# A recommendation tower in fp32: products of a batch in one run, dense inputs in unused places of the pairs, a small first load, most of the last batch's layer 1 ahead of its last products

## The chip, the cores and the metric

One Trainium2 chip, one of its cores. The metric is the device time of one execution in microseconds (us). "Before" ran three times: 175.21 us median, 174.92 to 176.21.

## What is computed

For each of 512 samples, 32 embedding rows of 256 numbers are looked up, all 496 dot products between them are taken, 16 dense inputs are appended, and three layers follow.

```python
e = jnp.stack([tbl_0[ids[:, 0]], ..., tbl_31[ids[:, 31]]], axis=1)   # 512 x 32 x 256
z = einsum('bnd,bmd->bnm', e, e)[:, iu, ju]                          # the pairs i < j, 496
h = jnp.concatenate([z, dense_ctx], axis=1)                          # 512 x 512
h = jnp.maximum(h @ W_top1 + b_top1, 0.0)                            # 512
h = jnp.maximum(h @ W_top2 + b_top2, 0.0)                            # 256
y = h @ W_top3                                                       # 1
```

## The kernel before

The samples are cut in 16 groups of 32 (n = 0 to 15); four groups are one batch b of 128 samples, for which the layers run.

**Look-ups.** The four smallest tables are looked up on PE: one-hot matmuls (`look_up`, L386) of the table's high and low parts; ACT keeps the result (`kept`). The other 28 tables are gathered by POOL: per group 7 indirect DMAs (L211) of 128 rows each, 112 in all, into a ring of 4 groups. The row numbers are `row_ids`, the sum (DVE, L219) of two arrays that one DMA loads at the start (`ids_sb`, L175, 112 KB).

**Fills.** `fill(n, u)` (L406), u = 0 to 3, transposes the rows of two gathers (one for u = 3) into one of three PSUM banks `xt_ps`; DVE (odd u) or ACT (even u) copies the bank to `xt`. PE waits for each gather by itself.

**Products.** `dots` (L429) multiplies the 32 x 32 products of the samples, eight bundles of four samples per group, each bundle four matmuls with 64 weight columns, alternately on the two halves of the array's columns. They go to `dots_ps`, two banks of two groups each ("a unit", v = n // 2). In the loop a group's products are spread: two bundles behind each of the next group's four fills (L502). Then `move` (DVE L246, 12 copies; ACT L311, 4) spreads a unit over `pairs`, which has the products as 8 columns j of 128 partitions x 128 samples.

**Layers.** For a batch, layer 1 is 4 chunks n of 128 outputs; each sums 8 matmuls over j (`pairs_part`, L440; weights 128 x 128, 128 sample columns) and one for the 16 dense inputs (`dense_part`, L435). Each fp32 matmul of the program stands as two records in the trace (the transposes as one). Layer 2 is 8 matmuls (L460), layer 3 is 2 (L468). The table `ROUND` says behind which fill of the 16 following ones each half chunk of layer 1 and the rest stand; `slots` turns group and fill into that number. All of it shares the bank `mlp_ps`.

**The end.** Behind the last fill stand half of layer 2 of batch 2, the products of group 15 in one run, the rest of layer 2 and layer 3; then the last batch: dense parts, then for k = 0 to 3 a chunk of layer 1 (16 records) followed by layer 2 of the chunk before it, each with a bank of its own; relu on ACT, the last relu on DVE (L272), layer 3, a copy (L326) and the store (L195). The moves of the last unit are made in two halves, one per group.

Each engine runs its own list in order; SP issues the loads, the weights into places of `small_sb` that the look-ups have left.

Of the kernel before, what the change touches and what calls it, by code (L numbers as in the profile page):

```python
# [32 lines left out]
DVE_QUADS = 3  # L33
FIRST = 4
# [6 lines left out]
def build_tower(nc, table, ids, small_tables, small_ids, chunk_rows, dense, w1, w1d, b1, w2, b2, w3, out):  # L41
# [7 lines left out]
    KR, CHUNKS = chunk_rows.shape  # L49
# [4 lines left out]
    with ExitStack() as ctx:  # L54
# [9 lines left out]
        ids_sb = sb("ids_sb", [P, 2, NM * GATHERS], I32)  # L64
# [3 lines left out]
        chunk_rows_sb = sb("chunk_rows_sb", [KR, CHUNKS])  # L68
# [14 lines left out]
        dense_sb = sb("dense_sb", [dense.shape[0], B])  # L83
        w1d_sb = sb("w1d_sb", [dense.shape[0], H1])
# [18 lines left out]
        last_l1_ps = [bank[:, 0:BLOCK] for bank in (*xt_ps, mlp_ps)]  # L103
        last_l2_ps = [bank[:, 0:BLOCK] for bank in found_ps[0]]
        last_l3_ps = found_ps[1][0][0:1, 0:BLOCK]
# [4 lines left out]
        chunk_rows_in = sem("chunk_rows_in")  # L110
# [43 lines left out]
        def moves(v, s, groups=(0, UNIT * GROUPS)):  # L154

            low_g, high_g = groups
            b, at = v // UNIT, s * Q + v % UNIT * UNIT * GROUPS
            for q in range(QUADS):
                col = s % 2 * N_FIELDS + q * JJ
                to = pairs[Q * q:Q * (q + 1), b % 2, :, at + low_g:at + high_g]  # L160
                source = dots_ps[v % 2][Q * s:Q * (s + 1), low_g:high_g, col:col + JJ]
# [11 lines left out]
        @block.sync  # L173
        def _(sp):
            sp.dma_start(ids_sb[:], ids).then_inc(ids_in, 16)  # L175
            for k in range(LOOKED_UP):
                if k:
                    sp.dma_start(small_ids_sb[:, k, :],
                                 small_ids[:, k, :].to_broadcast([KR, B])).then_inc(small_ids_in[k], 16)
                for c in range(0, CHUNKS, 2):  # L180
                    sp.dma_start(small_sb[:, k, c:c + 2, :],
                                 small_tables[k][:, c:c + 2, :]).then_inc(small_in[k][c // 2], 16)
            for to, source in ((b1_sb, b1), (b2_sb, b2), (w3_sb, w3)):
                sp.dma_start(to[:], source).then_inc(biases_in, 16)
            sp.dma_start(w1d_sb[:], w1d).then_inc(weights_in, 16)
            sp.dma_start(dense_sb[:], dense).then_inc(weights_in, 16)
# [6 lines left out]
            sp.dma_start(w2_sb[:], w2).then_inc(weights_in, 16)  # L193
            sp.wait_ge(y_ready, NB)
# [22 lines left out]
        def _(dve):  # L217
            dve.wait_ge(ids_in, 16)
            nc.vector.tensor_tensor(row_ids[:], ids_sb[:, 0, :], ids_sb[:, 1, :], ALU.add).then_inc(ids_ready, 1)  # L219
# [30 lines left out]
            dve.wait_ge(chunk_rows_in, 16)  # L250
            for two in range(TWOS):
                prepare(two)
            for f in range(len(FILL_BEHIND), FIRST * FILLS):
                take_xt(*divmod(f, FILLS))
# [21 lines left out]
        def _(act):  # L276
            act.dma_start(small_ids_sb[:, 0, :], small_ids[:, 0, :].to_broadcast([KR, B])).then_inc(small_ids_in[0], 16)
            act.dma_start(chunk_rows_sb[:], chunk_rows).then_inc(chunk_rows_in, 16)
# [70 lines left out]
            for n in range(FIRST + 1, NM):  # L349
                for u in range(FILLS):  # L350
                    take_xt(n, u)
                    if u == 1:
                        take_kept(n)
                        if n % 2 and n > FIRST + 1:
                            move((n - 3) // UNIT, range(DVE_QUADS, QUADS))
# [7 lines left out]
            v, b = NM // UNIT - 1, NB - 1  # L363
            move(v, range(DVE_QUADS, QUADS), (0, GROUPS))
            move(v, range(DVE_QUADS, QUADS), (GROUPS, UNIT * GROUPS))
            relu2(b - 1, loop_ps, range(N2))
# [7 lines left out]
        def _(pe):  # L374
# [35 lines left out]
            def dots(first, last):  # L410

                for n, g in (divmod(i, GROUPS) for i in range(first, last)):
                    v = n // UNIT
                    if g == 0:
                        on_act, on_dve = moved_fills(n, FILLS - 1)
                        pe.wait_ge(xt_act, on_act)
                        if on_dve:
                            pe.wait_ge(xt_dve, on_dve)
                        pe.wait_ge(kept_in_xt, n + 1)
                        if n % UNIT == 0 and v >= 2:  # L420

                            pe.wait_ge(moved_act, v - 1)
                            pe.wait_ge(moved_dve, v - 1)
# [7 lines left out]
                    if g == GROUPS - 1:  # L431
                        done.then_inc(dots_done, 1)

            def dense_part(b, n, banks, start=False):
                return nc.tensor.matmul(banks[n], w1d_sb[:, n * P:(n + 1) * P],  # L435
                                        dense_sb[:, b * BLOCK:(b + 1) * BLOCK], start=start, stop=not start)

            def pairs_part(b, n, columns, banks, start=True, stop=False):
                for j in columns:
                    done = nc.tensor.matmul(banks[n], w1_sb[:, j, n * P:(n + 1) * P], pairs[:, b % 2, j, :],  # L440
                                            start=(start and j == 0), stop=(stop and j == JJ - 1))
                return done

            def pairs_complete(b):
                more = b == NB - 1
                pe.wait_ge(moved_dve, 2 * (b + 1) + more)
                pe.wait_ge(moved_act, 2 * (b + 1) + more)

            def layer1_half(b, i):
                if i == 0:  # L450
                    pairs_complete(b)
# [3 lines left out]
                pairs_part(b, i // 2, range(i % 2 * JJ // 2, (i % 2 + 1) * JJ // 2), loop_ps)  # L455
                if i % 2:
                    dense_part(b, i // 2, loop_ps).then_inc(l1_done, 1)
# [33 lines left out]
            between = FIRST * FILLS - len(FILL_BEHIND)  # L491
            for i in range(between):
                fill(*divmod(len(FILL_BEHIND) + i, FILLS))
                dots(2 * GROUPS * i // between, 2 * GROUPS * (i + 1) // between)
            for u in range(FILLS):
                fill(FIRST, u)
                dots(2 * GROUPS + 4 * u, 2 * GROUPS + 4 * (u + 1))
            pe.wait_ge(weights_in, 16 * (JJ + 3))
# [5 lines left out]
            m, last = NB - 2, NB - 1  # L504
            dots((NM - 1) * GROUPS, NM * GROUPS)
            for u in range(FILLS):
                mlp(NM, u)
            for k in range(N1 - 1):
                dense_part(last, k, last_l1_ps, start=True)
            pairs_complete(last)  # L510
            pe.wait_ge(y_ready, last)
            dense_part(last, N1 - 1, last_l1_ps, start=True)
            for k in range(N1 + 1):
                if k < N1:
                    pairs_part(last, k, range(JJ), last_l1_ps, start=False, stop=True).then_inc(l1_done, 1)
                if k:
                    pe.wait_ge(h1_ready, last * N1 + k)
                    for n in range(N2):
                        layer2(n, k - 1, last_l2_ps)
            layer3(last, last_l3_ps)  # L520
# [62 lines left out]
```

## Time and profile before

| | us |
|---|---|
| median of three runs | 175.21 (174.92 to 176.21) |
| the profiled execution, its own time | 174.41 |
| its span, first to last instruction | 172.6 |
| PE busy | 153.7 (89%) |
| POOL busy | 110.5 (64%) |
| DVE, ACT busy | 68.6, 60.1 |

PE is TensorE's matmuls, PEld its weight loads, DVE VectorE, ACT ScalarE, POOL GpSimd, SP SyncE. Rows of a timeline are start us, duration us, engine, line, operation, output<-input, shapes, count, and in brackets the idle time before it and what ended it. Ends of matmuls are modelled: the records of a run overlap, so a run's pace is read from starts or from the chain of waits. The granted clock is TensorE's, as a share of 2.4 GHz.

### The profile page before, as it was taken

Reading aid. Unit: us, or ns where it says so; the run is one execution under the profiler, and the core shown is the slowest. Engines: PE = TensorE matmul, PEld = TensorE weight load, DVE = VectorE, ACT = ScalarE, POOL = GpSimd, SP = SyncE. Lnnn points to the kernel's source line nnn. Section 1 sums busy time; section 2 is a strip of 40 time slices with the busy share of each in tenths; the row PEclk is TensorE's granted clock in tenths of the full one; section 3 lists DMA queues with packets and bytes.
Section 4 is the critical chain, followed back from the end, with each engine's and each line's share of the span. In section 5 each row is a group of like instructions: output and inputs, shape, how many; then the busy total and the mean of one; then the engine's idle time right before and its main releaser. Section 6 shows DMA issues by size and latency. Waiting matters only on the chain.

```text
span 172.6 us, 4109 instructions
## 1 busy us (share of the span) xinstructions
PE 153.7 (89%) x1744; PEld 126.7 (73%) x1744; DVE 68.6 (40%) x186; ACT 60.1 (35%) x140; POOL 110.5 (64%) x118
## 2 busy tenths in 40 slices
PE   0199999998799999999998799999777999998993
PEld 0178888885588878888785587888545888887991
DVE  0699794600111892135216401640164015457000
ACT  2542848353623350114344121035251200453111
POOL 1677887777777777777777777777777777400000
PEclk9999999999789999999999999999999999999999
DMA  4999999643333334343433333333433333300000
GB/s 128 325 390 376 327 348 338 216 116 99 113 105 106 112 102 115 95 119 97 112 105 104 109 104 112 98 118 92 121 96 110 106 102 115 91 4 0 4 0 2
DMA packets 10356, 23.01 MB, mean 133 GB/s; under 512 B 2881, under 2 KB 3009, under 8 KB 10338
## 3 DMA queue, kind: packets, MB, share of 16 engines
q0 software_dynamic: 5376, 14.69, 29.0%
q1 hardware_dynamic: 4674, 7.79, 13.3%
q10 hardware_dynamic: 288, 0.27, 0.6%
q8 instruction: 14, 0.23, 0.5%
q14 instruction: 4, 0.03, 0.1%
HBM read 22.73 MB, written 0.00 MB: 132 GB/s over the span
## 4 chain that ended last, share of the span: by engine, by line
PE 67%; POOL 12%; DMA 6%; DVE 6%; issue 5%; ACT 4%; ACTq 0%; DVEq 0%
PE dots_ps L386 18%; PE mlp_ps L440 14%; PE dots_ps L429 12%; PE xt_ps L406 12%; POOL rows L211 12%; DVE pairs L246 4%; DMA rows<-table,row_ids 4%; PE xt_ps L440 3%; DMA chunk_rows_sb<-chunk_rows 3%; PE mlp_ps L435 3%; PE mlp_ps L460 2%; ACT h L317 1%; PE dots_ps L460 1%; ACT kept L289 1%; ACT xt L295 1%
## 5 line engine op out<-in xcount | busy, mean ns | idle before, releaser
L211 POOL DMA_INDIRECT rows<-table,row_ids x112 | 109.8, 980 | 37.7 <-issue 31.4
L295 ACT COPY xt<-xt_ps 128x512 f32<-128x512 f32 (+1 forms) x36 | 20.8, 577 | 81.4 <-PE xt_ps L406 81.4
L236 DVE COPY xt<-xt_ps 128x512 f32<-128x512 f32 (+1 forms) x28 | 15.6, 558 | 77.5 <-PE xt_ps L406 77.4
L406 PE MATMUL xt_ps<-ident,rows 128*128 128x128 f32 x224 | 39.4, 287 | 6.9 <-DMA rows<-table,row_ids 4.8
L429 PE MATMUL dots_ps<-xt 128*64 128x64 f32 x1024 | 43.0, 230 | 0.0
L429 PEld LDWEIGHTS dots_ps<-xt 128*64 128x64 f32 x1024 | 35.2, 140 | 9.5 <-issue 9.4
L406 PEld LDWEIGHTS xt_ps<-ident,rows 128*128 128x128 f32 x224 | 25.1, 143 | 14.3 <-DMA rows<-table,row_ids 5.9
L246 DVE COPY pairs<-dots_ps 32x128 f32<-32x128 f32 (+1 forms) x108 | 29.1, 269 | 3.2 <-PE dots_ps L429 1.7
L440 PE MATMUL mlp_ps<-pairs,small_sb 128*128 128x128 f32 x208 | 29.8, 287 | 0.3 <-DVE pairs L246 0.3
L386 PE MATMUL dots_ps<-one_hot,high 128*128 128x512 f32 x64 | 21.6, 420 | 7.8 <-DVE low L230 7.8
L440 PEld LDWEIGHTS mlp_ps<-pairs,small_sb 128*128 128x128 f32 x208 | 25.1, 191 | 2.0 <-DVE pairs L246 0.5
L386 PE MATMUL dots_ps<-one_hot,low 128*128 128x512 f32 x64 | 20.5, 402 | 0.0
L386 PEld LDWEIGHTS dots_ps<-one_hot,high 128*128 128x128 f32 x64 | 11.8, 197 | 9.8 <-issue 7.8
L226 DVE TENSOR_SCALAR one_hot<-small_ids_sb,chunk_rows_sb 128x512 fp32r<-128x512 int32 x32 | 14.6, 497 | 1.0 <-DMA chunk_rows_sb<-chunk_rows 1.0
L386 PEld LDWEIGHTS dots_ps<-one_hot,low 128*128 128x128 f32 x64 | 12.6, 197 | 2.9
L230 DVE TENSOR_TENSOR low<-small_sb,high 128x512 fp32r<-128x512 f32 x16 | 10.9, 683 | 4.5 <-ACT high L284 4.5
L284 ACT CAST high<-small_sb 128x512 fp32r<-128x512 f32 x16 | 9.7, 622 | 4.7 <-DMA small_sb<-small_tables 4.5
L311 ACT COPY pairs<-dots_ps 32x128 f32<-32x128 f32 (+1 forms) x36 | 8.9, 248 | 4.8 <-PE dots_ps L429 4.3
L289 ACT COPY kept<-dots_ps 128x512 f32<-128x512 f32 x8 | 8.0, 1104 | 4.8 <-PE dots_ps L386 4.8
L460 PE MATMUL mlp_ps<-h,small_sb 128*128 128x128 f32 x48 | 7.0, 288 | 0.4
L460 PEld LDWEIGHTS mlp_ps<-h,small_sb 128*128 128x128 f32 x48 | 5.8, 191 | 1.0 <-ACT h L317 0.8
L301 ACT COPY xt<-kept 128x256 f32<-128x256 f32 x16 | 6.2, 406 | 0.0
(27 smaller groups left out, 42.0 us busy)
## 6 DMA issues: line engine op xcount, KB each, us to landing
small_sb<-small_tables SPq DMA_DIRECT2D x16, 256.0 KB, 7.4
small_sb<-w SPq DMA_DIRECT2D x8, 256.0 KB
rows<-table,row_ids POOLq DMA_INDIRECT x112, 2.8
small_ids_sb<-small_ids SPq DMA_DIRECT2D x3, 256.0 KB, 7.3
small_sb<-w SPq DMA_DIRECT2D x1, 512.0 KB
small_ids_sb<-small_ids ACTq DMA_DIRECT2D x1, 256.0 KB, 4.4
ids_sb<-ids SPq DMA_DIRECT2D x1, 112.0 KB, 4.0
w1d_sb<-w1d SPq DMA_DIRECT2D x1, 32.0 KB
```

The source lines that it names most:

```text
L211: nc.gpsimd.indirect_dma_start(rows[:, slot, :], None, table, bass.IndirectOffsetOnAxis(ap=row_ids[:, m * GATHERS + t:m * GATHERS + t + 1] ...
L226: nc.vector.tensor_scalar(one_hot[:, i, :], small_ids_sb[:, k, :], chunk_rows_sb[:, c:c + 1], None, ALU.is_equal).then_inc(one_hot_ready, 1)
L230: nc.vector.tensor_tensor(low[:, k, c - 1:c + 1, :], small_sb[:, k, c - 1:c + 1, :], high[:, k, c - 1:c + 1, :], ALU.subtract).then_inc(lo ...
L236: nc.vector.tensor_copy(*fill_parts(n, u)).then_inc(xt_dve, 1)
L246: done = nc.vector.tensor_copy(to, source)
L289: last = nc.scalar.copy(kept[:, c, :, k], found_ps[k % 2][c])
L295: nc.scalar.copy(*fill_parts(n, u)).then_inc(xt_act, 1)
L386: last = nc.tensor.matmul(found_ps[k % 2][d], part[:, k, c, d * P:(d + 1) * P], one_hot[:, i, :], start=(c == 0 and part is high), stop=(c ...
L406: last = nc.tensor.transpose(xt_ps[at_fill % 3][:, at:at + P], rows[:, slot, c * P:(c + 1) * P], ident[:])
L429: done = nc.tensor.matmul(to[TILE * h:TILE * (h + 1), :], x, x, start=(c == 0), stop=(c == DC - 1))
L440: done = nc.tensor.matmul(banks[n], w1_sb[:, j, n * P:(n + 1) * P], pairs[:, b % 2, j, :], start=(start and j == 0), stop=(stop and j == J ...
L460: done = nc.tensor.matmul(banks[n], w2_sb[:, k, n * P:(n + 1) * P], h1[:, k, :], start=(k == 0), stop=(k == N1 - 1))
```

## The change

1. **Dense inputs.** Pair column j = 0 of the first quadrant (partitions 0 to 31) is a place that no product i < j needs. DVE zeroes it at the start, SP loads the dense inputs of a batch there (batches 2 and 3 later, behind `l1_done`), `w1` has the dense weights there, and the moves skip it. `dense_part` and its loads are gone; a chunk of layer 1 is 8 matmuls.
2. **Products.** `dots(n)` is one run of 32 matmuls (64 records), in the loop behind the first fill of the next group. The moves follow at every even group; layer 1 of batches 1 and 2 starts behind the fourth fill of that group (`ROUND` starts at 0, `slots` shifts by 3).
3. **Start.** SP's first load has the chunk rows and the ids of the first group alone (11 KB); the others' ids follow behind the first part of the first table, and DVE adds them behind its first `prepare`. POOL waits twice.
4. **Last batch.** Its pairs of groups 12 to 14 (96 of 128 sample columns) go through all of layer 1 (32 matmuls) behind the third fill of group 15; behind the last products the other 32 columns do, again with all 32 weight blocks. Layer 2 follows in one piece. The moves of the last group are split evenly, 8 on DVE and 8 on ACT; the banks are other ones.

```diff
+LAST_QUADS = range(2), range(2, QUADS)
-ROUND = {"layer1": [2, 3, 4, 5, 6, 7, 8, 9], "relu1": 10, "layer2": [11, 12], "relu2": 13, "layer3": 14, "keep": 15}
+DOTS_BEHIND = [10, 13]
+ROUND = {"layer1": [0, 1, 2, 3, 4, 5, 6, 7], "relu1": 8, "layer2": [9, 10], "relu2": 11, "layer3": 12, "keep": 13}
...
-                at = (n - (BATCHES * b + FIRST + 1)) * FILLS + u
+                at = (n - BATCHES * (b + 1)) * FILLS + u - (FILLS if b == 0 else FILLS - 1)
...
-            sp.dma_start(ids_sb[:], ids).then_inc(ids_in, 16)
+            sp.dma_start(first_sb[:], first_ids).then_inc(first_in, 16)
...
+                    if k == c == 0:
+                        sp.dma_start(ids_sb[:], ids).then_inc(ids_in, 16)
...
-            pool.wait_ge(ids_ready, 1)
             for m in range(NM):
+                if m < 2:
+                    pool.wait_ge(ids_ready, m + 1)
...
+            nc.vector.memset(pairs[0:Q, :, 0, :], 0.0).then_inc(no_pairs_zeroed, 1)
+            dve.wait_ge(first_in, 16)
+            nc.vector.tensor_tensor(row_ids[:, 0:GATHERS], first_ids_sb[:, 0, :], first_ids_sb[:, 1, :],
+                                    ALU.add).then_inc(ids_ready, 1)
...
                     take_xt(n, u)
-                    if n % 2 and n > FIRST + 1:
-                        if u == 0:
-                            move((n - 3) // UNIT, range(2), last=False)
+                    if n % UNIT == 0:
                         if u == 1:
-                            move((n - 3) // UNIT, range(2, DVE_QUADS), first=False)
+                            move(n // UNIT - 1, range(2), last=False)
+                        if u == 2:
+                            move(n // UNIT - 1, range(2, DVE_QUADS), first=False)
+                    if n == NM - 1 and u == 1:
+                        move(n // UNIT, range(DVE_QUADS), (0, GROUPS))
+            move(NM // UNIT - 1, LAST_QUADS[0], (GROUPS, UNIT * GROUPS))
...
                     fill(n, u)
-                    dots((n - 1) * GROUPS + 2 * u, (n - 1) * GROUPS + 2 * u + 2)
+                    if u == 0:
+                        dots(n - 1)
                     mlp(n, u)
+                    if n == NM - 1 and u == FILLS - 2:
+                        b = NB - 1
+                        pe.wait_ge(moved_dve, UNIT * (b + 1))
+                        pe.wait_ge(moved_act, UNIT * (b + 1))
+                        pe.wait_ge(dense_in, 16 * (b + 1))
+                        for k in range(N1):
+                            pairs_part(b, k, range(JJ), last_l1_ps, lambda x: last_batch(x, others))
+            dots(NM - 1)
+            mlp(NM, 0)
+            pe.wait_ge(moved_dve, UNIT * (b + 1) + 1)
+            pe.wait_ge(moved_act, UNIT * (b + 1) + 1)
+            for k in range(N1):
+                pairs_part(b, k, range(JJ), last_l1_ps, lambda x: last_batch(x, last_one)).then_inc(l1_done, 1)
+            for k in range(N1):
+                if k % 2 == 0:
+                    pe.wait_ge(h1_ready, b * N1 + k + 2)
+                for n in range(N2):
+                    layer2(n, k, last_l2_ps)
+            layer3(b, last_l3_ps)
```

PE's list in the loop, around the start of a batch's layer 1 (transposes write `xt_ps`, products `dots_ps<-xt`, layer 1 `mlp_ps<-pairs`, the dense part `w1d_sb`). Before:

```order
L406 MATMUL xt_ps<-ident,rows 128x128 x4
L429 MATMUL dots_ps<-xt 64x64 x8
L440 MATMUL mlp_ps<-pairs,small_sb 128x128 x4
L406 MATMUL xt_ps<-ident,rows 128x128 x2
L429 MATMUL dots_ps<-xt 64x64 x8
L440 MATMUL mlp_ps<-pairs,small_sb 128x128 x4
L435 MATMUL mlp_ps<-dense_sb,w1d_sb 128x128
```

After, the same place (other line numbers):

```order
L435 MATMUL xt_ps<-ident,rows 128x128 x4
L456 MATMUL dots_ps<-xt 64x64 x32
L462 MATMUL mlp_ps<-pairs,small_sb 128x128 x4
L435 MATMUL xt_ps<-ident,rows 128x128 x4
L462 MATMUL mlp_ps<-pairs,small_sb 128x128 x4
L435 MATMUL xt_ps<-ident,rows 128x128 x4
```

Four product runs of 8 matmuls became one of 32, and the dense matmuls left. PE's list at the end, from the products of group 14 on. Before:

```order
L429 MATMUL dots_ps<-xt 64x64 x8
L460 MATMUL mlp_ps<-h,small_sb 128x128 x4
L429 MATMUL dots_ps<-xt 64x64 x32
L460 MATMUL mlp_ps<-h,small_sb 128x128 x4
L468 MATMUL mlp_ps<-h,w_sb 1x128 x2
L435 MATMUL xt_ps<-dense_sb,w1d_sb 128x128 x3
L435 MATMUL mlp_ps<-dense_sb,w1d_sb 128x128
L440 MATMUL xt_ps<-pairs,small_sb 128x128 x16
L460 MATMUL dots_ps<-h,small_sb 128x128 x2
L440 MATMUL xt_ps<-pairs,small_sb 128x128 x8
L460 MATMUL dots_ps<-h,small_sb 128x128 x2
L440 MATMUL mlp_ps<-pairs,small_sb 128x128 x8
```

After:

```order
L456 MATMUL dots_ps<-xt 64x64 x32
L485 MATMUL mlp_ps<-h,small_sb 128x128 x4
L435 MATMUL xt_ps<-ident,rows 128x128 x4
L485 MATMUL mlp_ps<-h,small_sb 128x128 x4
L435 MATMUL xt_ps<-ident,rows 128x128 x4
L462 MATMUL dots_ps<-pairs,small_sb 128x4x24 x32
L435 MATMUL xt_ps<-ident,rows 128x128 x2
L493 MATMUL mlp_ps<-h,w_sb 1x128 x2
L456 MATMUL dots_ps<-xt 64x64 x32
L462 MATMUL dots_ps<-pairs,small_sb 128x4x8 x32
L485 MATMUL xt_ps<-h,small_sb 128x128 x8
L493 MATMUL xt_ps<-h,w_sb 1x128 x2
```

The 32 matmuls of layer 1 stand twice now, once with 4 x 24 sample columns ahead of the last fill and the last products, once with 4 x 8 behind them.

## Rows read from the trace of the kernel before

**Rows 1.** The page: busy us (share of the span) xinstructions
```profile
PE 153.7 (89%) x1744; PEld 126.7 (73%) x1744; DVE 68.6 (40%) x186; ACT 60.1 (35%) x140; POOL 110.5 (64%) x118
```

**Rows 2.** Source line of the gathers, whole span
```profile
L211 POOL DMA_INDIRECT rows<-table,row_ids x112: 942/947/1525, 5.4 to 148.0; - x112
...
DMA to landing us min/median/max: 2.7/2.8/6.9
```

**Rows 3.** The chain that ended last: start us, us, what
```profile
71.04 0.61 PE dots_ps L429 x16
71.66 1.09 PE mlp_ps L440 x8
72.74 0.41 PE mlp_ps L435 x2
...
100.50 3.51 DMA rows<-table,row_ids
...
129.26 2.71 DMA rows<-table,row_ids
...
154.35 2.02 PE dots_ps L429 x64
...
159.85 3.77 PE xt_ps L440 x32
...
164.07 1.79 PE xt_ps L440 x16
...
168.55 0.72 PE dots_ps L460 x4
```

**Rows 4.** Timeline, a move in the loop and the end of the span
```profile
57.29 3.56 DVE L246 COPY pairs<-dots_ps 32x128 f32<-32x128 f32 x12
...
148.02 0.94 POOL L211 DMA_INDIRECT rows<-table,row_ids  x1 [0.30 <-issue]
...
148.81 0.69 DVE L236 COPY xt<-xt_ps 128x512 f32<-128x512 f32 x1 [1.86 <-PE xt_ps L406]
...
152.02 0.44 PE L406 MATMUL xt_ps<-ident,rows 128*128 128x128 f32 x2
...
153.12 2.76 DVE L246 COPY pairs<-dots_ps 32x64 f32<-32x64 f32 x12 [0.20 <-PE dots_ps L429]
...
156.42 0.86 ACT L311 COPY pairs<-dots_ps 32x64 f32<-32x64 f32 x4 [2.39 <-PE dots_ps L429]
```

**Rows 5.** Timeline of PEld, windows 154.28:154.36, 159.7:159.9 and 170.1:170.2
```profile
154.28 0.20 PEld L429 LDWEIGHTS dots_ps<-xt 128*64 128x64 f32 x4
...
159.78 0.30 PEld L440 LDWEIGHTS xt_ps<-pairs,small_sb 128*128 128x128 f32 x2
...
170.14 0.09 PEld L468 LDWEIGHTS dots_ps<-h,w_sb 128*1 128x1 f32 x2 [1.07 <-DVE h L272]
```

**Rows 6.** Stretches: us, busy of five engines, PEclk, DMA share, GB/s; timeline of PE
```profile
44.00:46.00 2.00, 1.57 (x20) 1.35 (x20) 0.69 (x1) 1.70 (x5) 1.48 (x2) 0.75 0.28 82
...
46.00:48.00 2.00, 2.00 (x24) 1.60 (x20) 0.00 (x0) 0.59 (x1) 1.39 (x3) 0.50 0.35 115
...
48.00:50.00 2.00, 2.00 (x32) 1.46 (x30) 0.42 (x1) 0.05 (x1) 1.69 (x2) 0.89 0.41 109
...
130.00:132.00 2.00, 1.05 (x19) 0.71 (x18) 1.84 (x5) 0.00 (x0) 1.39 (x3) 1.00 0.31 96
...
44.43 0.66 PE L406 MATMUL xt_ps<-ident,rows 128*128 128x128 f32 x4 [2.04 <-ACT kept L289]
...
124.17 0.44 PE L406 MATMUL xt_ps<-ident,rows 128*128 128x128 f32 x2 [1.06 <-DMA rows<-table,row_ids]
```

**Rows 7.** The start: chain, timeline of DVE, one stretch
```profile
1.17 4.88 DMA chunk_rows_sb<-chunk_rows
...
4.81 0.28 DVE L219 CUSTOM_DVE_ANT_0 row_ids<-ids_sb 128x224 uint16<-128x224 uint16 x1 [4.81 <-DMA ids_sb<-ids]
...
1.75:2.00 0.25, 0.00 (x0) 0.00 (x0) 0.00 (x0) 0.25 (x1) 0.00 (x0) 1.00 1.19 121
```

More of the change, by code:

```diff
@@ L33, with build_tower @@
 DVE_QUADS = 3
+LAST_QUADS = range(2), range(2, QUADS)
 FIRST = 4
 FILL_BEHIND = [2, 4, 5, 7, 8, 10, 11, 13, 14]
-ROUND = {"layer1": [2, 3, 4, 5, 6, 7, 8, 9], "relu1": 10, "layer2": [11, 12], "relu2": 13, "layer3": 14, "keep": 15}
-def build_tower(nc, table, ids, small_tables, small_ids, chunk_rows, dense, w1, w1d, b1, w2, b2, w3, out):
+DOTS_BEHIND = [10, 13]
+ROUND = {"layer1": [0, 1, 2, 3, 4, 5, 6, 7], "relu1": 8, "layer2": [9, 10], "relu2": 11, "layer3": 12, "keep": 13}
+def build_tower(nc, table, first_ids, ids, small_tables, small_ids, dense, w1, b1, w2, b2, w3, out):
     D = table.shape[1]
@@ L48, in build_tower @@
     N1, N2 = H1 // P, H2 // P
-    KR, CHUNKS = chunk_rows.shape
+    KR, CHUNKS = small_tables.shape[1:3]
     assert KR == P
@@ L102, in build_tower @@
         loop_ps = [mlp_ps[:, n * BLOCK:(n + 1) * BLOCK] for n in range(N1)]
-        last_l1_ps = [bank[:, 0:BLOCK] for bank in (*xt_ps, mlp_ps)]
-        last_l2_ps = [bank[:, 0:BLOCK] for bank in found_ps[0]]
-        last_l3_ps = found_ps[1][0][0:1, 0:BLOCK]
+        last_l1_ps = [found_ps[0][n // 2][:, n % 2 * BLOCK:(n % 2 + 1) * BLOCK] for n in range(N1)]
+        last_l2_ps = [bank[:, 0:BLOCK] for bank in xt_ps[0:N2]]
+        last_l3_ps = xt_ps[N2][0:1, 0:BLOCK]
+        first_in = sem("first_in")
         ids_in = sem("ids_in")
@@ L182, in _, with load_dense @@
                                  small_tables[k][:, c:c + 2, :]).then_inc(small_in[k][c // 2], 16)
+                    if k == c == 0:
+                        sp.dma_start(ids_sb[:], ids).then_inc(ids_in, 16)
             for to, source in ((b1_sb, b1), (b2_sb, b2), (w3_sb, w3)):
                 sp.dma_start(to[:], source).then_inc(biases_in, 16)
-            sp.dma_start(w1d_sb[:], w1d).then_inc(weights_in, 16)
-            sp.dma_start(dense_sb[:], dense).then_inc(weights_in, 16)
+            def load_dense(b):
+                sp.dma_start(pairs[0:dense.shape[0], b % 2, 0, :],
+                             dense[:, b * BLOCK:(b + 1) * BLOCK]).then_inc(dense_in, 16)
+            sp.wait_ge(no_pairs_zeroed, 1)
+            load_dense(0)
+            load_dense(1)
             assert H1 % D == 0 and H2 == D
@@ L193, in _ @@
             sp.dma_start(w2_sb[:], w2).then_inc(weights_in, 16)
+            for b in range(2, NB):
+                sp.wait_ge(l1_done, N1 * (b - 1))
+                sp.wait_ge(dense_in, 16 * b)
+                load_dense(b)
             sp.wait_ge(y_ready, NB)
@@ L248, in move @@
                     done.then_inc(moved_dve, 1)
-            dve.wait_ge(chunk_rows_in, 16)
             for two in range(TWOS):
                 prepare(two)
+                if two == 0:
+                    more_row_ids()
             for f in range(len(FILL_BEHIND), FIRST * FILLS):
@@ L353, in _ @@
                         take_kept(n)
-                        if n % 2 and n > FIRST + 1:
-                            move((n - 3) // UNIT, range(DVE_QUADS, QUADS))
+                        if n % UNIT == 0:
+                            move(n // UNIT - 1, range(DVE_QUADS, QUADS))
+                        if n == NM - 1:
+                            move(n // UNIT, range(DVE_QUADS, QUADS), (0, GROUPS))
                     for b, at in slots(n, u):
@@ L362, in _ @@
                             keep_y(b, loop_ps[0][0:1, :])
[L363 to L366, printed above, removed]
+            b = NB - 1
             keep_y(b - 1, loop_ps[0][0:1, :])
-            for k in range(N1):
-                relu1(b, last_l1_ps, [k])
+            move(NM // UNIT - 1, LAST_QUADS[1], (GROUPS, UNIT * GROUPS))
+            for k in range(0, N1, 2):
+                relu1(b, last_l1_ps, range(k, k + 2))
             relu2(b, last_l2_ps, range(N2 - 1))
@@ L408, in fill, with dots @@
                 last.then_inc(transposed, 1)
[L410 to L423, printed above, removed]
+            def dots(n):
+                v = n // UNIT
+                on_act, on_dve = moved_fills(n, FILLS - 1)
+                pe.wait_ge(xt_act, on_act)
+                if on_dve:
+                    pe.wait_ge(xt_dve, on_dve)
+                pe.wait_ge(kept_in_xt, n + 1)
+                if n % UNIT == 0 and v >= 2:
+                    pe.wait_ge(moved_act, v - 1)
+                    pe.wait_ge(moved_dve, v - 1)
+                for g in range(GROUPS):
                     to = dots_ps[v % 2][:, n % UNIT * GROUPS + g, :]
@@ L430, in dots, with pairs_part, last_batch @@
                                                     start=(c == 0), stop=(c == DC - 1))
[L431 to L438, printed above, removed]
+                done.then_inc(dots_done, 1)
+            def pairs_part(b, n, columns, bank, pick=lambda x: x):
                 for j in columns:
-                    done = nc.tensor.matmul(banks[n], w1_sb[:, j, n * P:(n + 1) * P], pairs[:, b % 2, j, :],
-                                            start=(start and j == 0), stop=(stop and j == JJ - 1))
-                return done
[L444 to L447, printed above, removed]
+                    done = nc.tensor.matmul(pick(bank[n]), w1_sb[:, j, n * P:(n + 1) * P], pick(pairs[:, b % 2, j, :]),
+                                            start=(j == 0), stop=(j == JJ - 1))
+                return done
             def layer1_half(b, i):
                 if i == 0:
-                    pairs_complete(b)
+                    pe.wait_ge(moved_dve, UNIT * (b + 1))
+                    pe.wait_ge(moved_act, UNIT * (b + 1))
+                    pe.wait_ge(dense_in, 16 * (b + 1))
                     if b:
                         pe.wait_ge(y_ready, b)
-                pairs_part(b, i // 2, range(i % 2 * JJ // 2, (i % 2 + 1) * JJ // 2), loop_ps)
+                done = pairs_part(b, i // 2, range(i % 2 * JJ // 2, (i % 2 + 1) * JJ // 2), loop_ps)
                 if i % 2:
-                    dense_part(b, i // 2, loop_ps).then_inc(l1_done, 1)
+                    done.then_inc(l1_done, 1)
+            def last_batch(x, taken):
+                return x.rearrange("p (s c) -> p s c", s=GROUP)[:, :, taken]
+            others, last_one = slice(0, BLOCK // GROUP - GROUPS), slice(BLOCK // GROUP - GROUPS, BLOCK // GROUP)
             def layer2(n, k, banks):
@@ L490, in _ @@
             pe.wait_ge(found_kept, LOOKED_UP)
[L491 to L494, printed above, removed]
+            for f in range(len(FILL_BEHIND), FIRST * FILLS):
+                fill(*divmod(f, FILLS))
+                if f in DOTS_BEHIND:
+                    dots(DOTS_BEHIND.index(f))
             for u in range(FILLS):
                 fill(FIRST, u)
-                dots(2 * GROUPS + 4 * u, 2 * GROUPS + 4 * (u + 1))
-            pe.wait_ge(weights_in, 16 * (JJ + 3))
+                if u % 2 == 0:
+                    dots(len(DOTS_BEHIND) + u // 2)
+            pe.wait_ge(weights_in, 16 * (JJ + 1))
             for n in range(FIRST + 1, NM):
@@ L501, in _ @@
                     fill(n, u)
-                    dots((n - 1) * GROUPS + 2 * u, (n - 1) * GROUPS + 2 * u + 2)
+                    if u == 0:
+                        dots(n - 1)
                     mlp(n, u)
[L504 to L520, printed above, removed]
+                    if n == NM - 1 and u == FILLS - 2:
+                        b = NB - 1
+                        pe.wait_ge(moved_dve, UNIT * (b + 1))
+                        pe.wait_ge(moved_act, UNIT * (b + 1))
+                        pe.wait_ge(dense_in, 16 * (b + 1))
+                        for k in range(N1):
[12 more added lines that the diff above has]
+            layer3(b, last_l3_ps)
 def kernel(**inputs):
```

35 lines of the change are left out of this document (18 added, 17 removed).

## The prediction

> **How the profile was read, and what bounds the kernel.** The span is 172.6 us, the profiled execution 174.41 us, so 1.8 us lie outside the span; the median of the three runs is 175.21 us, 0.8 us more. I make the sum against 172.6 and 174.41.
>
> The busy line comes first: PE 89%, POOL 64% [rows 1]. But POOL's work is one instruction kind, 112 gathers, the first at 5.4 us and the last at 148.0 us [rows 2]; for each of its gathers the engine takes 0.95 us and 0.30 us of idle time labelled as issue. From the gather that starts at 129.26 us to the last at 148.02 us there are 15, so one starts every 1.25 us [rows 3, 4]. The stream never pauses. Data land 2.8 us after the start (median, 2.7 at least; [rows 2]). Twice the chain of waits leaves PE and runs back along POOL, ending in a landing [rows 3]. So there are two bounds: a gather stream that nothing in PE can shorten, and PE's work in the layer 1 stages. At the end they nearly coincide: the last gather lands about 148.02 + 2.8 = 150.8 us, PE's last transposes start at 152.02 us [rows 4]. PE lags the stream by 1.2 us, and no more can be won by a faster PE inside the loop. Everything after 152 us is a serial tail of 20.6 us: products, moves out of PSUM, layer 1 of the last batch, layers 2 and 3, store. The change is decided by what it does to that tail.
>
> **In the loop.** The split product run of 16 records takes 0.61 us, so four take 2.44 us; the one run of 64 records took 2.02 us [rows 3]. A full-array group behind a product run costs 1.09 us against 8 x 0.112 = 0.90 us from the row of 16 records in 1.79 us, so each switch that goes saves 0.19 us [rows 3]. The dense matmul of a chunk, 0.41 us for two records [rows 3], goes: its weights and inputs now sit in the unused j = 0 place. Per batch PE then needs 4 x (2.02 + 0.19) + 28 gathers x 2 transposes x 0.11 + 64 x 0.112 + 16 x 0.112 + 0.6 = 8.8 + 6.2 + 7.2 + 1.8 + 0.6 = 24.6 us, while 28 gathers take 35.0 us. Wait added: layer 1 of a batch now starts three fills behind the last products of its pairs. DVE needs 0.69 us for a bank's copy and 3.56 us for its 12 moves [rows 4], 4.3 us behind the products; the third of those fills waits for gathers that land 5 x 1.25 us after the ones ahead of the products, 6.25 us, of which the products take some 2.3. So PE stands about 4.3 + 2.3 - 6.25 - 0.3 = 0.1 us, with the next fill's transposes queued behind it. Cost: nothing, covered by the 10 us of slack per batch; without that cover 0.1 to 1 us per batch. So in the loop PE loses its lag of 1.2 us and stands waiting for gathers.
>
> **The start.** POOL begins when the ids have been loaded and added: the load ends at 4.81 us [rows 7]. The first load shrinks from 112 KB to 11 KB. Bounds: bytes begin to flow in the slice at 1.75 us [rows 7], so at most 2.8 us are won; a load of only 4 KB took 4.88 us [rows 7], by which 0.8 us would be lost. The small load stays first on its queue, beside the same 256 KB of small ids on the other. I take 1.0 us, nearer to the big load's own row than to either end, and 0.2 us for the add that now covers 14 columns instead of 224 (0.28 us). The whole gather stream shifts by s = 1.2 us (bounds -0.8 to 3.0). The second ids load, the memset and the two small dense loads lie beside DVE and SP work that starts long before anyone needs them: nothing.
>
> **The tail, step by step** (times of the kernel before's gather stream; s comes off at the end). The gathers of the last group start at 148.02 - 6 x 1.25 = 140.52 us. (1) The second lands at 144.6, its transposes end at 144.85. (2) Products of group 14 in one run, 2.1 us: 146.95. (3) Half of layer 2 with the switch, 1.09: 148.05; transposes 0.44: 148.5. (4) DVE now has the copy of that bank, 0.69 us, and then 12 half moves, 2.76 us [rows 4]: it is done at 148.57 + 0.69 + 0.03 + 2.76 = 152.05 us. (5) Meanwhile PE has done the other half of layer 2 and the third fill (its gather lands at 149.6) and stands from about 149.85 to 152.1 us for the new wait on these moves. Behind it are queued the last fill, layer 3 of the batch before, the last products. (6) Then 32 matmuls of 96 columns, 64 records. What does a record with fewer columns cost?
>
> This is the term that decides. Before each matmul its weights are loaded. At the start of a burst of 128-column weights two loads span 0.30 us, each 0.19 us long, so the second starts 0.11 us behind the first, though no matmul is finished by then; with weights of one column two loads span 0.09 us, each 0.08 us: 0.01 us apart. Four loads of 64 columns, two to each half of the array, span 0.20 us [rows 5]. So a load holds up the next by about 0.11 us for 128 columns, whatever the matmul does. In the tail of before both the load and the 128 columns take 0.11 us, and 16 records take 1.79 us [rows 3], 0.112 each. Cutting the matmul's columns to 96 or 32 doesn't cut its weights, which stay at 128 columns. So (6) costs 64 x 0.112 = 7.2 us: 159.3 us, and the same weights are loaded a second time for the last quarter. Bounds for a record: 0.112 us at the top; at the bottom the moving columns, 0.112 x 96/128 = 0.084 us here, and 0.112 x 32/128 = 0.028 us for the last quarter; between them, if loads go by the product run (2.02 us over 64 records of 64 weight columns, 0.032 each), 2 x 0.032 = 0.063 us. I take the top, since the row of two loads shows exactly this weight shape.
>
> (7) The last two transposes, 0.22: 159.5; layer 3, 0.45, covers most of DVE's copy of the last bank (0.42 us); products from 160.15, 2.05 us: 162.2. (8) Moves: eight each on DVE and ACT. Twelve took 2.76 and four 0.86 [rows 4], so 8 x 0.23 = 1.85: PE goes on at 164.1 us. (9) 64 records again, 0.112: 171.3. (10) Layer 2 in one piece, 16 records: 15 x 0.112 + 0.27 and 0.05 for the relu = 2.0: 173.3. (11) From the end of layer 2 (168.55 + 0.72 = 169.27, [rows 3]) to the end of the span before, 3.33 us, unchanged: 176.6 us. Minus s: 175.4 us, 2.8 us more than 172.6. In short: layers 1 and 2 of the last batch took from 159.85 to 169.27 [rows 3], 9.4 us, and take 9.2 us behind the last moves now; what was to be ahead of the last batch isn't ahead of anything, because the last gather but one lands at 149.6 and the last at 150.8: 7.2 us of matmuls stand in a place where only some 1 us is free.
>
> The Trainium skill has the same price as a rule: "TensorE: Matmul & The Clock Gate", section "LDWEIGHTS (loading the stationary operand)", gives weight columns divided by 1.2 ns, whatever the contraction. For 128 columns that is 107 ns; the trace agrees with its 0.11 us between the two loads. It speaks against the change; by it step (6) and (9) would cost 64 x 0.107 = 6.8 us each.
>
> **The clock.** After the one long PE gap in the trace, 2.04 us before 44.43, the granted clock fell to 0.75 and 0.50 of full in the next slices (1.2 GHz of 2.4); a gap of 1.06 us before 124.17 didn't do that [rows 6]. The work lost over three slices of 2 us, at 0.75, 0.50 and 0.89, is 2 x 0.25 + 2 x 0.50 + 2 x 0.11 = 1.7 us. The changed kernel has two such gaps on its path, 2.25 us before step (6) and 1.9 us before step (9). Bounds 0 and 3.4 us; I take one of them, 1.7 us, since both are as long as the gap that did it, but follow denser work. Span 177.1 us, time 178.9 us.
>
> **The rivals.**
> A. Matmuls of fewer columns are faster, which is what the change needs. Records at 0.084 and 0.028 us: (6) 5.4, (9) 2.0 with the last one's latency; 1.8 + 5.2 = 7.0 us less, 168.4 without the clock's loss, 170.2 us as a time. With 0.063 us in (9): 5.4 and 4.0, 172.2 us. For it: nothing in the trace has few columns on 128-column weights, so the overlap is only inferred from burst starts. Against it: [rows 5]. This is the case on the other side, faster; it turns at about 0.09 us per record in both steps. The same skill page, section "Back-to-back issue gap", gives the moving columns over 2.4 plus 2.5 ns for isolated matmuls with no load: by that rule 32 columns are far below 0.112 us; its own text adds that loads must be counted where each matmul has one, and the trace bears out that part.
> B. The load sets the pace, but the small terms go well: ids land 2.5 us earlier, no loss by the clock. 176.6 - 2.7 + 1.8 = 175.7 us, no change that can be told.
> C. PE's new waits in the loop (layer 1 behind the moves) together with a half clock in the sparse stretches make PE late at the last group: 24.6 us of work at half clock would be 49 us against 35. For it: between batches the new order leaves PE idle for some 2 us per fill. Against it: from 130 to 132 us PE was busy 1.05 of 2 us at full clock [rows 6]. With two more us at the end: 181 us.
>
> **How the numbers follow.** Forecast 0.70, C 0.05, both slower by over 1% (a percent, 1.75 us, is about what a measurement of this kernel can tell from no change); B and what lies near it 0.11; A 0.14. So faster 0.14, same 0.12, slower 0.74. The likeliest case alone runs from 176.0 (no clock loss, s = 2.4) to 181.5 us (both losses, s = 0.3). The stated range adds B and the upper part of A: 172.2 to 181.5 us.
>
> **What would show it.** Right: POOL's gathers 1.25 us apart from about 4.2 us, last at about 146.8; layer 1 of the last batch as two groups of 64 records, some 7 us each, both with loads 0.11 us apart; a PE wait of about 2 us for DVE's moves ahead of each; a lower granted clock behind one of them. Wrong: if the second group takes 2 to 4 us, the load floor is refuted and A holds; if PE's wait ahead of the first is gone, step (4) fails; if the first gather starts later than 5.4 us, the start term has the wrong sign.

## The result, and the profile after

The changed kernel takes 185.16 us (median of 4, 184.14 to 186.07) against 175.06 us (4 runs, 173.4 to 176.21): ratio 1.061, 95% interval 1.051 to 1.071. It was forecast slower, at 178.9 us with a range up to 181.5 us: the direction holds, the size doesn't. The profiled execution took 185.24 us, its span is 183.3 us against 172.6.

The page, the same line as [rows 1], and the granted clock in 40 slices:

```profile
PE 153.9 (84%) x1776; PEld 136.7 (75%) x1776; DVE 66.5 (36%) x184; ACT 60.3 (33%) x144; POOL 109.5 (60%) x118
...
PEclk9999999999999999999569999996999996996558
```

PE's busy time is unchanged, in a span 10.7 us longer. Each digit of PEclk is the granted clock of one of 40 equal slices, in tenths, and these digits are where to look: dips in the loop, one near 152 us, and a long one at the end.

The chain of waits at the end (start us, us, what) answers to the working of the tail:

```profile
150.89 9.01 PE dots_ps L462 x64
159.90 0.22 PE xt_ps L435 x2
160.12 0.53 PE mlp_ps L493 x4
160.68 2.10 PE dots_ps L456 x64
...
164.66 12.36 PE dots_ps L462 x64
177.02 3.36 PE xt_ps L485 x16
180.48 0.36 DVE h L302
```

Both passes of layer 1 stand on the chain. The one of 96 columns starts at 150.89 us, behind DVE's moves, and takes 9.0 us; the one of 32 columns takes 12.4 us, a third of the columns and longer; layer 2 takes 3.4 us, where 2.0 was worked out.

Two short windows of the weight loads within the last pass, and stretches of it (us, busy of PE, PEld, DVE, ACT, POOL, then PEclk, DMA share, GB/s):

```profile
164.88 0.41 PEld L462 LDWEIGHTS dots_ps<-pairs,small_sb 128*128 128x128 f32 x3
...
169.72 0.76 PEld L462 LDWEIGHTS dots_ps<-pairs,small_sb 128*128 128x128 f32 x3
```

```profile
158.00:160.00 2.00, 2.00 (x20) 1.88 (x18) 0.00 (x0) 0.00 (x0) 0.00 (x0) 1.00 0.00 0
166.00:168.00 2.00, 2.00 (x13) 2.00 (x12) 0.00 (x0) 0.00 (x0) 0.00 (x0) 0.58 0.00 0
168.00:170.00 2.00, 2.00 (x11) 2.00 (x11) 0.00 (x0) 0.00 (x0) 0.00 (x0) 0.50 0.00 0
176.00:178.00 2.00, 2.00 (x10) 2.00 (x11) 0.00 (x0) 0.63 (x2) 0.00 (x0) 0.50 0.00 0
```

Three loads span 0.41 us, each 0.19 us long, so they start 0.11 us apart, with matmuls of 32 columns beside them: the load sets the pace. Then PEclk is 0.50 and three loads span 0.76 us, each 0.33 us long: 0.21 us apart. Of the pass, the first 1.7 us ran at full clock and the rest at half, with PE never idle. All four executions of this kernel had a mean granted clock of 0.90 to 0.93; the kernel before had 0.99 in its profile.

The gather stream (start us, us): its first start moved from 5.37 to 5.22 us only, its last from 148.02 to 146.94.

```profile
5.22 1.10 POOL L232 DMA_INDIRECT rows<-table,row_ids  x1 [3.75 <-DVE row_ids L242]
...
19.04 0.94 POOL L232 DMA_INDIRECT rows<-table,row_ids  x1 [0.30 <-issue]
...
146.94 0.95 POOL L232 DMA_INDIRECT rows<-table,row_ids  x1 [0.30 <-issue]
```

### The profile page after: what moved, and what is told of

It reads as the page before. It is cut to its first block, busy times and chain, and to the rows that moved or that the text cites. A ratio compares the mean times of both kernels' runs of the same rounds, so it can differ in the third digit from the quotient of the medians.

```text
span 183.3 us, 4181 instructions
## 1 busy us (share of the span) xinstructions
PE 153.9 (84%) x1776; PEld 136.7 (75%) x1776; DVE 66.5 (36%) x184; ACT 60.3 (33%) x144; POOL 109.5 (60%) x118
## 4 chain that ended last, share of the span: by engine, by line
PE 60%; POOL 11%; DMA 10%; DVE 10%; issue 5%; ACT 2%; SPq 0%; DVEq 0%
PE dots_ps L415 18%; PE dots_ps L462 12%; PE dots_ps L456 11%; POOL rows L232 11%; PE xt_ps L435 10%; DMA rows<-table,row_ids 8%; DVE pairs L275 8%; PE mlp_ps L462 6%; DMA small_sb<-small_tables 2%; PE xt_ps L485 2%; PE mlp_ps L485 2%; DVE xt L265 1%; ACT kept L318 1%; DVE low L259 0%; ACT high L313 0%
## 5 line engine op out<-in xcount | busy, mean ns | idle before, releaser
L435 PE MATMUL xt_ps<-ident,rows 128*128 128x128 f32 x224 | 36.9, 285 | 11.0 <-DMA rows<-table,row_ids 8.9
L435 PEld LDWEIGHTS xt_ps<-ident,rows 128*128 128x128 f32 x224 | 26.3, 145 | 16.9 <-issue 4.1
L456 PEld LDWEIGHTS dots_ps<-xt 128*64 128x64 f32 x1024 | 33.1, 144 | 6.0 <-issue 3.2
L456 PE MATMUL dots_ps<-xt 128*64 128x64 f32 x1024 | 35.1, 230 | 2.8 <-DVE xt L265 1.4
L462 PE MATMUL mlp_ps<-pairs,small_sb 128*128 128x128 f32 x192 | 27.2, 286 | 2.5 <-DVE pairs L275 2.5
L275 DVE COPY pairs<-dots_ps 32x112 f32<-32x112 f32 (+3 forms) x104 | 27.7, 267 | 3.5 <-PE dots_ps L456 2.2
L462 PE MATMUL dots_ps<-pairs,small_sb 128*128 128x96 f32 (+1 forms) x128 | 21.4, 343 | 3.9 <-DVE pairs L275 3.9
L462 PEld LDWEIGHTS dots_ps<-pairs,small_sb 128*128 128x128 f32 x128 | 21.1, 263 | 4.2 <-DVE pairs L275 4.2
L255 DVE TENSOR_SCALAR one_hot<-small_ids_sb,first_sb 128x512 fp32r<-128x512 int32 x32 | 14.1, 486 | 0.0
L340 ACT COPY pairs<-dots_ps 32x128 f32<-32x128 f32 (+3 forms) x40 | 9.6, 240 | 10.4 <-PE dots_ps L456 10.0
```

Of the source, the lines that this page charges most:

```text
L255: nc.vector.tensor_scalar(one_hot[:, i, :], small_ids_sb[:, k, :], chunk_rows_sb[:, c:c + 1], None, ALU.is_equal).then_inc(one_hot_ready, 1)
L275: done = nc.vector.tensor_copy(to, source)
L435: last = nc.tensor.transpose(xt_ps[at_fill % 3][:, at:at + P], rows[:, slot, c * P:(c + 1) * P], ident[:])
L456: done = nc.tensor.matmul(to[TILE * h:TILE * (h + 1), :], x, x, start=(c == 0), stop=(c == DC - 1))
L462: done = nc.tensor.matmul(pick(bank[n]), w1_sb[:, j, n * P:(n + 1) * P], pick(pairs[:, b % 2, j, :]), start=(j == 0), stop=(j == JJ - 1))
```

## The experiments

Here "the pass ahead" is layer 1 over 96 columns ahead of the last fill, "the last pass" the one behind the last products. Theories: T1, a record costs its weight load, and a pass of few-column matmuls runs at half clock by itself; T2, only the idle gaps ahead of the passes lower the clock; and, against both, that the pace goes by columns. Line diffs are against the changed kernel unless said otherwise.

**e1, one pass.** The pass ahead is taken out, the last one has all columns.

```diff
-                    if n == NM - 1 and u == FILLS - 2:
...
-                            pairs_part(b, k, range(JJ), last_l1_ps, lambda x: last_batch(x, others))
...
-                pairs_part(b, k, range(JJ), last_l1_ps, lambda x: last_batch(x, last_one)).then_inc(l1_done, 1)
+                pairs_part(b, k, range(JJ), last_l1_ps).then_inc(l1_done, 1)
```

> The changed kernel without the pass ahead: layer 1 of the last batch is 64 records once, with all 128 columns, behind the last moves. Work: nothing left out. Load floor theory (each record costs its 128-column weight load, 0.112 us, whatever the columns): the last gather lands at 149.7, products end at 152.6, moves at 154.5, layer 1 7.2 (8.9 with one stretch at half clock), layer 2 2.0, the rest 3.3: span 167.0 to 168.7, time 169 to 170.6 us, faster than both kernels. If instead the pass ahead had hidden work in free PE time, its removal would cost: 185 us or more.

169.9 us (169.18 to 171.35), ratio to before 0.973 (0.967 to 0.978): faster than both kernels. Span 169.5; its timeline has one pass of 9.0 us with a stretch at half clock, and layer 2 in 2 us:

```profile
155.61 9.01 PE L462 MATMUL dots_ps<-pairs,small_sb 128*128 128x128 f32 x64 [1.94 <-DVE pairs L275]
164.46 2.04 PE L485 MATMUL xt_ps<-h,small_sb 128*128 128x128 f32 x16
```

So the pass ahead, with the narrow last pass that comes with it, costs 15 us and hides nothing. The rest of the change is a gain.

**e2, last pass over 128 columns.** The pass ahead stays, only the last one changes.

```diff
-                pairs_part(b, k, range(JJ), last_l1_ps, lambda x: last_batch(x, last_one)).then_inc(l1_done, 1)
+                pairs_part(b, k, range(JJ), last_l1_ps).then_inc(l1_done, 1)
```

> The changed kernel, but the last pass computes all 128 columns again instead of the last 32 (the pass ahead stays, its result is overwritten): 4 times the columns, the same 64 loads. Theory T1 (matmuls of few columns keep the granted clock low): the clock recovers within the last pass as it did in the pass of 96 columns, so the pass takes about 9 us instead of 12.4 and layer 2 2 us instead of 3.5: time about 180 us, faster with more work. Theory T2 (only the PE gap ahead sets the clock): the last pass takes 12.4 us as before, 185 us. Column pace theory: slower than 185 us.

178.4 us (177.8 and 179.0; ratio 1.023, 1.015 to 1.031). Four times the columns in the same 64 loads, and 6.7 us less than the changed kernel. The gap ahead is the same, yet the pass runs at full clock:

```profile
164.87 7.41 PE L462 MATMUL dots_ps<-pairs,small_sb 128*128 128x128 f32 x64 [1.89 <-DVE pairs L275]
```

```profile
166.00:168.00 2.00, 2.00 (x21) 2.00 (x20) 0.00 (x0) 0.00 (x0) 0.00 (x0) 1.00 0.03 8
```

The mean clock was 0.96 and 0.97 in the two executions, against 0.90 to 0.93. Column pace is refuted. T2's 12.4 us didn't come either, but e3 shows that such a gap lowers the clock in some executions only, so what decides on T2 is e4.

**e3, last pass over 64 columns.**

```diff
+            last_two = slice(BLOCK // GROUP - 2 * GROUPS, BLOCK // GROUP)
...
-                pairs_part(b, k, range(JJ), last_l1_ps, lambda x: last_batch(x, last_one)).then_inc(l1_done, 1)
+                pairs_part(b, k, range(JJ), last_l1_ps, lambda x: last_batch(x, last_two)).then_inc(l1_done, 1)
```

> As the changed kernel, the last pass over 64 columns (group 14's again and group 15's). T1: between the pass of 32 columns (12.4 us, clock never back) and the one of 96 (9.0 us, back after 3.4 us); 180 to 185 us. T2: 12.4 us.

One run: 183.9 us. The last pass took 12.96 us: its clock was 0.60 from 164 to 166 us and 0.50 from there to its end, like that of the pass of 32. The pass ahead of 96 columns, behind a gap of 2.1 us, took 7.4 us here, at full clock throughout: such a gap lowers the clock in some executions only.

```profile
151.18 7.38 PE L462 MATMUL dots_ps<-pairs,small_sb 128*128 128x96 f32 x64 [2.09 <-DVE pairs L275]
...
163.34 12.96 PE L462 MATMUL dots_ps<-pairs,small_sb 128*128 128x64 f32 x64 [1.90 <-DVE pairs L275]
```

**e4, no gaps.** Eight added matmuls (16 records of 128 columns, result unused) ahead of each of the two waits for the moves, into an unused quarter of a bank.

```diff
+            def filler():
+                for j in range(JJ):
+                    nc.tensor.matmul(found_ps[0][0][:, 3 * BLOCK:4 * BLOCK], w1_sb[:, j, 0:P], w1_sb[:, j, 0:P], start=(j == 0), stop=(j == JJ - 1))
...
                         b = NB - 1
+                        pe.wait_ge(moved_dve, UNIT * (b + 1) - 1)
+                        pe.wait_ge(moved_act, UNIT * (b + 1) - 1)
+                        filler()
...
             mlp(NM, 0)
+            filler()
```

> The changed kernel with 8 added matmuls (16 records of 128 columns, 1.8 us, result unused) in each of the two PE gaps ahead of the passes. T2 (the gaps alone lower the clock): both passes at 7.2 us, layer 2 2 us: span about 175, time 177 us. T1 (narrow matmuls lower it by themselves): the pass ahead takes 7.2 us, the last one starts at full clock and falls within it, 10 to 11 us, layer 2 still 3.5 us: time 181 to 183 us.

One run: 182.75 us. The pass ahead took 7.4 us. The last one started at full clock with no gap before it and fell within it:

```profile
150.50 7.38 PE L462 MATMUL dots_ps<-pairs,small_sb 128*128 128x96 f32 x64
...
160.68 2.05 PE L512 MATMUL dots_ps<-small_sb 128*128 128x128 f32 x16
162.65 11.22 PE L462 MATMUL dots_ps<-pairs,small_sb 128*128 128x32 f32 x64
173.69 3.76 PE L485 MATMUL xt_ps<-h,small_sb 128*128 128x128 f32 x16
```

```profile
162.00:164.00 2.00, 2.00 (x19) 1.89 (x18) 0.57 (x3) 0.47 (x3) 0.00 (x0) 1.00 0.00 0
164.00:166.00 2.00, 2.00 (x18) 2.00 (x18) 0.00 (x0) 0.00 (x0) 0.00 (x0) 0.90 0.00 0
166.00:168.00 2.00, 2.00 (x11) 2.00 (x11) 0.00 (x0) 0.63 (x2) 0.00 (x0) 0.50 0.00 0
```

T2 is refuted: with PE busy without a gap the clock still fell, 2.9 us into the narrow pass, and layers 2 and 3 behind it still ran at half. The pass ahead, 96 columns on the same loads behind the same filler, stayed at full clock.

**e9, e4 with the narrow pass over neighbouring columns.** It computes other samples than those of group 15; the work is the same.

```diff
-                pairs_part(b, k, range(JJ), last_l1_ps, lambda x: last_batch(x, last_one)).then_inc(l1_done, 1)
+                pairs_part(b, k, range(JJ), last_l1_ps, lambda x: x[:, BLOCK - GROUP * GROUPS:]).then_inc(l1_done, 1)
```

> Control for e4_no_gap: the last pass covers 32 neighbouring columns (96 to 127) in place of 4 pieces of 8; which samples it computes is wrong by this, so the output is not the reference's. If the number of columns keeps the clock low: falls within the pass, 11 us, span about 181, 183 us. If the strided access did it: the pass takes 7.2 us at full clock, 176.5 us.

One run: 184.3 us, the pass 11.17 us, half clock from about 167 us, 3 us into it:

```profile
166.00:168.00 2.00, 2.00 (x17) 2.00 (x16) 0.00 (x0) 0.00 (x0) 0.00 (x0) 0.81 0.00 0
168.00:170.00 2.00, 2.00 (x11) 2.00 (x11) 0.00 (x0) 0.63 (x2) 0.00 (x0) 0.50 0.00 0
```

The pieces of 8 columns are not the cause.

**e10, the kernel before with narrow matmuls in its last pass.** `pick` is applied to the output and to the moving columns, as in the changed kernel.

```diff
-                    pairs_part(last, k, range(JJ), last_l1_ps, start=False, stop=True).then_inc(l1_done, 1)
+                    pairs_part(last, k, range(JJ), last_l1_ps, start=False, stop=True, pick=lambda x: x[:, 0:BLOCK // 4]).then_inc(l1_done, 1)
```

> The kernel before with layer 1 of the last batch over 32 of its 128 columns in the matmuls of the pairs: three quarters of that work are left out, the 64 weight loads stay. Load floor: no time is saved, 174.5 us; if narrow matmuls lower the clock by themselves, some 4 to 6 us are lost on top, 178 to 181 us. Column pace: 5 us less, 169 us.

182.3 us (2 runs), ratio 1.040 (1.033 to 1.047): three quarters of the columns left out, 7 us lost; I had expected at most 6. The chunks behind the first took 3.3 us from start to start of what follows, against 1.79 [rows 3], at half clock:

```profile
161.84 4.91 PE L440 MATMUL xt_ps<-pairs,small_sb 128*128 128x32 f32 x32
...
167.55 3.46 PE L440 MATMUL xt_ps<-pairs,small_sb 128*128 128x32 f32 x16
```

```profile
162.00:164.00 2.00, 2.00 (x20) 2.00 (x20) 0.00 (x0) 0.15 (x1) 0.00 (x0) 1.00 0.00 0
164.00:166.00 2.00, 2.00 (x13) 2.00 (x12) 0.00 (x0) 0.22 (x1) 0.00 (x0) 0.55 0.04 8
166.00:168.00 2.00, 2.00 (x11) 2.00 (x11) 0.00 (x0) 0.37 (x1) 0.00 (x0) 0.50 0.00 0
```

**e8, both passes, full clock**: e4's edit and e2's. **e5, one pass, no gap**: e1's edit, e4's `filler`, and

```diff
             b = NB - 1
             pe.wait_ge(dense_in, 16 * (b + 1))
+            pe.wait_ge(moved_dve, UNIT * (b + 1) - 1)
+            pe.wait_ge(moved_act, UNIT * (b + 1) - 1)
+            filler()
```

> e4_no_gap with the last pass over all 128 columns: both passes at 64 loads, no gap ahead of either, no narrow matmul. Theory: full clock throughout, passes of 7.2 us each, layer 2 2 us: span about 175.0, time 176.5 us. Less e5_one_pass_no_gap it is the pure price of the pass ahead, 6 to 7 us. Rival: a clock loss remains, 178 us.

> e1_one_pass with 8 added matmuls (16 records of 128 columns, result unused) in the 1.9 us gap ahead of layer 1. e1's layer 1 took 8.85 us with one stretch at half clock. Theory: the clock stays full, layer 1 takes 7.2 us, span 167.9, time 168.3 us in the median. Rival: the clock falls anyway, or the added matmuls end after the moves, 169.9 us or more.

e8: 177.7 us (177.4 and 178.0; ratio 1.018, 1.006 to 1.030); passes of 7.4 us each and clock 1.00 in the tail; 1.2 us above the expectation, since the pass ahead came later, at 151.67. The reason lies in the loop: in this profile the granted clock was 0.50 from 124 to 130 us, and PE, behind the gather stream, worked without a wait from 128 us on and came to group 14's products late:

```profile
144.63 2.09 PE L456 MATMUL dots_ps<-xt 128*64 128x64 f32 x64 [1.13 <-ACT xt L324]
...
151.67 7.39 PE L462 MATMUL dots_ps<-pairs,small_sb 128*128 128x96 f32 x64 [0.31 <-DVE pairs L275]
...
163.82 7.41 PE L462 MATMUL dots_ps<-pairs,small_sb 128*128 128x128 f32 x64
```

The products start 1.9 us ahead of the last gather here, 3.1 us ahead of it in the changed kernel (143.85 and 146.94).

e5: 169.8 us (169.49 to 171.31), ratio 0.976 (0.965 to 0.986). In its profile the pass takes 7.4 us in place of e1's 9.0, but the medians don't differ: whether the filler gains anything is not shown. e8 less e5 is 7.9 us: the price of the pass ahead at full clock, some 1.2 us of it the delay from the loop that e8's profile shows.

**e6, e1 with the loads of the start as before.**

```diff
-            sp.dma_start(first_sb[:], first_ids).then_inc(first_in, 16)
+            sp.dma_start(ids_sb[:], ids).then_inc(ids_in, 16)
...
+            act.dma_start(chunk_rows_sb[:], chunk_rows).then_inc(first_in, 16)
```

**e7, the kernel before with only the dense inputs in the pairs and the small first load.** Products, moves, `ROUND` and the end stand as before; for example

```diff
-                    if u == 0:
-                        dots(n - 1)
+                    dots((n - 1) * GROUPS + 2 * u, (n - 1) * GROUPS + 2 * u + 2)
```

> e1_one_pass with the loads of the start as before (all ids in one load of 112 KB first, the chunk rows on ACT's queue). Theory: the gather stream, which bounds the end, starts and paces as before, its last gather at 148.0 instead of 146.9: 1.1 us slower than e1, 171.0 us. Rival (the first load is hidden): 169.9 us.

> The kernel before with only the dense inputs in the pairs and the small first load; products in four runs, moves, tail with layer 2 interleaved as before. Theory: the shift of the gather stream (1.1 us) and the dense matmuls that go in the tail (0.5 us) and in the loop (PE's lag of 1.2 us at the last gather, part of it) are won: 171.5 to 172.7 us. Against e1 (169.9) the rest is what the one run and the one-piece tail bring, about 2 us. Rival (dense matmuls are covered by waits): 173.2 us.

e6: 171.0 us (0.979, 0.970 to 0.988), as expected 1.1 us above e1, but the intervals overlap. Its first gather starts at 6.39 us, its last at 147.60, 0.7 us behind that of the changed kernel. In this profile PE too is late at group 14's products (145.32 us, 2.3 us ahead of the last gather), so the 1.1 us aren't the loads' alone. e7: 171.8 us (0.983, 0.972 to 0.993), inside its range. So the dense inputs and the first load are worth about 1.7%; that the one run of products adds to it (e1 against e7, 1.9 us) is likely, but those intervals overlap too and e1's tail differs as well.

## Why the prediction was half right

**The loop.** Right: POOL's stream is the bound, 1.25 us per gather to 146.94 us, and PE waits for it. PE's waits for the moves ahead of layer 1 were up to 1.3 us, not 0.1, and the clock fell near 88 and 125 us; in this profile both are hidden by the slack, since the pass ahead still starts at the time worked out. That was in part luck: in the profiles of e2, e3, e8 and e9, with the same loop, the half clock near 125 us lasted some 7 us, in place of 3 to 4 in the changed kernel and e4; group 14's products came only 1.9 to 2.2 us ahead of the last gather in place of 3.1, and the pass ahead started at 151.1 to 152.1 us.

**The start.** The size was right (1.2 worked out, 1.08 measured), the reason wrong, so this is luck. The small load brought 0.15 us at the first gather; the rest came between: before, the eleventh gather started at 19.87 us, 14.5 us behind the first; now it starts at 19.04, 13.8 us behind it. That pace isn't the load's doing either: e6, with the load of before, has 13.9 us there, and e7, with the small one, 14.6. What sets it was not tried. Over all profiles the first gather starts at 5.05 to 5.63 us with the small load (9 kernels) and at 5.37 to 6.39 with the big one (3), the last at 145.97 to 147.17 and 147.60 to 148.02.

**Steps (1) to (5).** Right to 0.1 us: PE goes on at 152.1 - 1.2 = 150.9 us, measured 150.89.

**The load floor, steps (6) and (9).** Right: 64 records took 7.4 us at full clock with 96 columns (e3, e4) and with 128 (e2, e5), and with 32 the loads were 0.11 us apart. It is the reason for the sign. e8 less e5, 7.9 us, is its price with the 1.2 us of delay.

**The clock.** This is the step that failed: "Bounds 0 and 3.4 us; I take one of them, 1.7 us". It took the loss to come from gaps, each ending after one stretch. The one gap loss was there ahead of time (9.0 us for 7.2), and with it step (9) starts at 164.6, measured 164.66. But the last pass took 12.4 for 7.2 us and layer 2 3.4 for 2.0, because under the 32-column matmuls the clock was at half from 166.3 us to 180 us, nearly the end of layer 2, and the forecast had no term for that. 5.2 + 1.4, less 0.4 us that the end behind layer 2 was shorter, is 6.2 us: 177.1 becomes 183.3. The gap ahead may have its part in how early the clock fell (1.7 us into the pass; 2.9 in e4, without a gap, where the pass took 11.2 us); the two can't be told apart by one profile of each. Changed kernel less e2, the same loads with wide matmuls, is 6.7 us. So of 15.3 us that the pass ahead costs (185.2 less e1's 169.9), 8.5 are the pass ahead itself (e2 less e1: the loads paid twice, and about 1 us of delay from the loop in e2's profile) and 6.7 the clock.

**The rivals.** A fell on e2 and e10: pace doesn't go by columns. B (175.7) fell with the start, 0.15 us earlier for 2.5, and with the clock. C, the half clock in the loop, did come; it had room in the changed kernel's profile, and cost about 1 us in e2, e3, e8 and e9, where it lasted some 7 us.

The Trainium skill, "TensorE: Matmul & The Clock Gate", section "LDWEIGHTS (loading the stationary operand)", puts the load at 107 ns for 128 columns; the trace agrees, 0.11 us at full clock, even with 32 moving columns. The Trainium skill, same page, "Why this matters for your kernels", asks in its table for TensorE to be kept busy continuously, with no long idle gaps between bursts. By it e4's narrow pass would run at full clock, and e4 differs: PE busy 2.00 of 2 us and a clock of 0.50.

## What to carry to other kernels

Cutting the moving columns of these fp32 matmuls below their 128 weight columns saved nothing, since each record kept its 0.11 us of load: to split such work in two by columns pays all weight loads twice. Work put "ahead" must stand where the engine is idle, and here that was 1 us, not 7. And where a stage would consist of matmuls much narrower than their weights, read the granted clock of such a stage before counting on it: here doing the whole width was 6.7 us faster than a quarter of it.

## What had not been expected of the hardware

Back-to-back matmuls of 32 or 64 columns on 128-column fp32 weights, without any idle time of PE, ran at 1.2 GHz: the granted clock fell 2.4 to 3.0 us into the pass (e4, e9, e10) and stayed at 0.50 over the 128-column matmuls of layer 2 (16 records, 3.8 us for 2.0 in e4 and e9; 3.4 in the changed kernel; in e3 it came back within them, 3.0 us). Passes of 96 and 128 columns behind a gap of about 2 us either stayed at full clock (7.4 us: e2's last pass, e3's first, e6) or fell and came back within the pass (9.0 us: the changed kernel's first, e2's first, e1), three passes of each kind; what tells them apart stays open. Without a gap, or behind one of 0.3 us, they stayed at full clock (the first passes of e4 and e9, e5, both of e8).
